# A transformer block with 32 routed experts on one core: gathers that wait for true block counts, zeroed result rows, earlier additions, fewer clears

## The reference

```python
x = x + cross_attention(layernorm(x), ctx, ctx)          # 16 heads of 16
xf = layernorm(x).reshape(4096, 256)
scores = sigmoid(xf @ gate_w.T)                          # 32 experts
# the best 4 of 8 groups by score + bias, then the best 6 experts within them
w = scores[chosen] / sum(scores[chosen]) * 2.5
routed = sum over the 6 chosen e of w[e] * (silu(xf @ gate_e.T) * (xf @ up_e.T)) @ down_e.T
x = x + routed + shared_ffn(xf)
```

## Time and profile before

| what | value |
|---|---|
| time, median of 3 runs | 761.74 us (759.81 to 762.38) |
| the profiled execution: its own time | 759.98 us |
| the profiled execution: span | 758.2 us |
| TensorE busy | 714.4 us (94%) |
| VectorE busy | 520.7 us (69%) |
| ScalarE busy | 394.2 us (52%) |
| GpSimd busy | 534.7 us (71%) |
| mean granted TensorE clock | 0.974 |

### The profile page before, as it was taken

One profiled execution on the slowest core, in us unless ns is written; L12 is line 12 of the kernel. 1 busy time (PEld: TensorE's weight loads), 2 busy tenths in 40 slices (PEclk: granted clock), 3 DMA queues, 4 the chain that ended last, 5 costly groups with the idle time before them and its releaser, 6 DMA issues.

```text
span 758.2 us, 18389 instructions
## 1 busy us (share of the span) xinstructions
PE 714.4 (94%) x5864; PEld 649.7 (86%) x5864; DVE 520.7 (69%) x1628; ACT 394.2 (52%) x836; POOL 534.7 (71%) x778
## 2 busy tenths in 40 slices
PE   6899999999999999998899999999999999999960
PEld 3789898888998888887589999999999999999950
DVE  4997777777777777776834327777776676676663
ACT  2455455455555555531046666666666666666630
POOL 0126778788888888878800027889888888888884
PEclk9999999999999999997999999999999999999995
DMA  9313443344342234334575557888888888888862
GB/s 277 109 57 113 127 139 109 122 140 136 137 141 80 82 112 139 135 126 144 171 228 197 168 178 243 261 269 263 272 269 274 274 269 264 262 276 269 282 202 81
DMA packets 97294, 140.13 MB, mean 185 GB/s; under 512 B 14943, under 2 KB 69731, under 8 KB 97200
## 3 DMA queue, kind: packets, MB, share of 16 engines
q1 hardware_dynamic: 77112, 87.50, 35.8%
q0 software_dynamic: 18432, 50.36, 21.5%
q10 hardware_dynamic: 1656, 1.10, 0.5%
HBM read 75.98 MB, written 62.94 MB: 183 GB/s over the span
## 4 chain that ended last, share of the span: by engine, by line
PE 75%; POOL 10%; DVE 6%; DMA 4%; issue 3%; DVEq 0%; POOLq 0%; ACT 0%; SPq 0%
PE sc_ps L989 19%; PE bank L1001 9%; PE bank L805 9%; PE sc_ps L865 7%; POOL work L550 6%; PE bank L793 5%; PE sc_ps L973 4%; PE bank L826 4%; PE bank L751 4%; DMA work<-yrows,dest 3%; PE sc_ps L771 3%; POOL work L503 3%; PE sc_ps L889 3%; PE sc_ps L767 2%; PE bank L835 2%
## 5 line engine op out<-in xcount | busy, mean ns | idle before, releaser
L513 POOL DMA_INDIRECT rows<-work,dest x192 | 188.3, 981 | 51.4 <-issue 26.9
L989 PE MATMUL sc_ps<-work 128*128 128x128 f32 x1792 | 218.6, 275 | 0.8 <-DVE work L1478 0.8
L550 POOL DMA_INDIRECT work<-yrows,dest x192 | 189.1, 985 | 34.9 <-POOL work L503 27.7
L989 PEld LDWEIGHTS sc_ps<-work 128*128 128x128 f32 x1792 | 209.1, 192 | 1.1 <-ACT work L655 1.0
L503 POOL MEMSET work<- 128x304 f32 (+1 forms) x350 | 133.1, 380 | 74.2 <-DMA yrows<-work 72.1
L1001 PE MATMUL bank<-wdn,work 128*128 x448 | 115.5, 380 | 0.6 <-DVE work L1433 0.6
L1459 DVE SCALAR_TENSOR_TENSOR work<-work 128x256 f32<-128x256 f32 x160 | 77.0, 482 | 47.1 <-DMA work<-yrows,dest 44.7
L1433 DVE TENSOR_TENSOR work<-work,sc_ps 128x256 f32<-128x256 f32 x112 | 46.9, 419 | 73.2 <-ACT work L660 73.1
L681 ACT ACTIVATE work<-bank 128x512 f32<-128x512 f32 x112 | 66.9, 597 | 54.3 <-PE bank L1001 54.3
L1001 PEld LDWEIGHTS bank<-wdn,work 128*128 128x128 f32 x448 | 76.6, 191 | 6.8 <-issue 1.0
L655 ACT ACTIVATE work<-sc_ps 128x512 f32<-128x512 f32 x112 | 66.3, 592 | 25.8 <-PE sc_ps L973 25.8
(11 more groups left out here) (168 smaller groups left out, 1051.7 us busy)
## 6 DMA issues: line engine op xcount, KB each, us to landing
work<-rows SPq DMA_DIRECT2D x224, 128.0 KB
yrows<-work SPq DMA_DIRECT2D x112, 256.0 KB
wgu<-in_egu SPq DMA_DIRECT2D x16, 512.0 KB, 4.2
store<-in_x SPq DMA_DIRECT2D x8, 512.0 KB, 11.1
wdn<-in_edn SPq DMA_DIRECT2D x8, 512.0 KB, 4.4
rows<-padrow SPq DMA_DIRECT2D x8, 512.0 KB, 3.3
out<-work SPq DMA_DIRECT2D x32, 128.0 KB
rows<-work,dest POOLq DMA_INDIRECT x192
```

The costliest lines, as they stand in the source:

```text
L513: pool.indirect_dma_start(rows[:, :], bass.IndirectOffsetOnAxis(ap=dest[:, t, k:k + 1], axis=0), rowb[:, m, :], None).then_inc(scat[m], 16)
L550: pool.indirect_dma_start(yg[:, g % RG, :], None, yrows[0:2 * n * P, :], bass.IndirectOffsetOnAxis(ap=dest[:, t, k:k + 1], axis=0)).then_i ...
L989: last = mm(ps8[2 + m % 2][:, (2 * w + g) * P:(2 * w + g + 1) * P], wst[w][m % 2][:, k * 2 * I + g * I:k * 2 * I + (g + 1) * I], xeT[:, m ...
```

## The change

There are five edits.

1. **True counts.** One more small matmul sums `begun` over the experts, and `count_stored` on VectorE turns it into `table` entries: for each tile and each of the 4 `y_st` semaphores the count that says that every block begun by the end of that tile is stored. GpSimd loads 16 of them (4 tiles) at a time (`load_known`), and waits on the four registers ahead of a tile's first gather. The waits by `stored_before` go; the row range that a gather may read is the same.
2. **Zeroed rows.** From tile 4 to tile 27 of the first part, SP stores 1 MB of zeros (8 blocks of 128 rows, `FILL`) into `yrows`, blocks 32 to 223. SP waits for these 24 stores ahead of the expert loop.
3. **Additions from pair 21** (ADD0), in place of 24.
4. **No clears** ahead of the gathers of tiles 16 to 31 (96 gathers; before, only the 6 of tile 31 had none).
5. `table`, `codes` and the PSUM bank hold a little more.

```diff
--- before.py
+++ after.py
@@ -30,13 +30,14 @@
 YP = 4
 PARTS = (0, 4, 16, NT)
 RG = 10
-ADD0 = 24
+ADD0 = 21
 OUT0 = ADD0 + 3
 NPR = NTB // 2
 UA, UB = 4, 8
 WORK = 13056
 TS = 8
 NPL = (NT - TS) // 2
+FILL0, FILL = 32, 8
 CLEARS = TOPK * NT - (NT - 4)
 NX = NT - TS
 
@@ -164,7 +165,7 @@
         padrow = sb("padrow", [P, D])
 
         pc = sb("pc", [P, 2, E * NT // P])
-        table = sb("table", [1, 4 * P], i32)
+        table = sb("table", [1, 4 * P + YP * NT], i32)
 
         att = []
 
@@ -248,7 +249,7 @@
         run, at = carve(work, at, [P, 2, 2 * NT])
         apart, at = carve(work, at, [P, NT])
         thr, at = carve(work, at, [P, NT])
-        codes, at = carve(work, at, [P, 2 * P])
+        codes, at = carve(work, at, [P, 2 * P + YP * NT])
         codes = codes[0:1, :].bitcast(i32)
         assert at <= 12 * 256 + 3 * NCH * P
 
@@ -271,6 +272,7 @@
         cum_ps = bank[3][0:E, 0:NT + 1]
         pos_ps = bank[3][0:E, 64:64 + NT]
         sch_ps = bank[3][0:1, P:P + NTB]
+        begun_ps = bank[3][0:1, P + NTB:P + NTB + NT]
         VB = (4, 6, 7, 4, 6)
         ps8 = [sc_ps[:, i, :] for i in range(4)] + [b[:, :] for b in bank]
         vchunk = [ps8[VB[c // 2]][:, (c % 2) * B * 3 * DH:(c % 2 + 1) * B * 3 * DH] for c in range(NCH)]
@@ -289,6 +291,7 @@
 
         scat = [sem(f"scat{i}") for i in range(4)]
         pads_st = sem("pads_st")
+        fill_st = sem("fill_st")
         ld_xe = [sem(f"ld_xe{i}") for i in range(RX)]
         y_st = [sem(f"y_st{i}") for i in range(YP)]
         ld_y = [sem(f"ld_y{i}") for i in range(RG)]
@@ -349,6 +352,12 @@
                 table[0:1, row * P + j:row * P + j + n], engines=(engine,), min_val=0, max_val=top,
                 skip_runtime_bounds_check_because="the table's entries are clipped to this range where it is made")
             return got
+
+        def load_known(t, n):
+            at = 4 * P + t * YP
+            _, got = nc.values_load_multi_w_load_instructions(
+                table[0:1, at:at + n * YP], engines=(mybir.EngineType.Pool,), min_val=16, max_val=16 * NPR // YP)
+            return [got[i * YP:(i + 1) * YP] for i in range(n)]
 
         def stored_before(t):
             return min(NPR, -(-(((t + 1) * P * TOPK + E * (P - 1)) // P) // 2))
@@ -400,9 +409,16 @@
                     sp.dma_start(ahead[0:P, e0:e0 + 4, :],
                                  padrow[:, :].unsqueeze(1).broadcast_to([P, 4, D])).then_inc(pads_st, 16)
 
+            def st_zeros(t, m, s):
+                b0 = FILL0 + FILL * (t - 4)
+                if FILL0 <= b0 < NTB:
+                    sp.dma_start(yrows[b0 * P:(b0 + FILL) * P, :].rearrange("(p j) d -> p j d", p=P),
+                                 padrow[:, :].unsqueeze(1).broadcast_to([P, FILL, D])).then_inc(fill_st, 16)
+
             def step(tile):
                 at_tile(tile, 0, ld_experts)
                 at_tile(tile, 0, st_pads)
+                at_tile(tile, 0, st_zeros)
             over_tiles(step)
 
             def ld_behind(i):
@@ -420,6 +436,7 @@
                 ld_behind(i)
             sp.wait_ge(S_["table"], 2)
             sp.wait_ge(pads_st, 16 * E // 4)
+            sp.wait_ge(fill_st, 16 * ((NTB - FILL0) // FILL))
             for one in scat:
                 sp.wait_ge(one, 16 * TOPK * NT // 4)
             sp.wait_ge(S_["gap"], CLEARS)
@@ -532,25 +549,26 @@
                 at_tile(tile, 0, late_inverse)
             over_tiles(step)
 
+            known = []
+
             def gather(t):
                 n = stored_before(t)
+                if t % 4 == 0:
+                    known.extend(load_known(t, 4))
                 need(pool, "dest2", t)
+                for one, stored_by in zip(y_st, known[t]):
+                    pool.wait_ge(one, stored_by)
                 for k in range(TOPK):
                     g = t * TOPK + k
-                    if g == 0:
-                        for i in range(n - YP, n):
-                            pool.wait_ge(y_st[i % YP], 16 * (i // YP + 1))
-                    elif k % 2 == 0 and n - 1 + k // 2 < NPR:
-                        i = n - 1 + k // 2
-                        pool.wait_ge(y_st[i % YP], 16 * (i // YP + 1))
                     if g >= RG:
                         need(pool, "part", g - RG)
-                    if t < NT - 1:
+                    if t < NT - 16:
                         gap(spare)
                     pool.indirect_dma_start(yg[:, g % RG, :], None, yrows[0:2 * n * P, :],
                                             bass.IndirectOffsetOnAxis(ap=dest[:, t, k:k + 1], axis=0)
                                             ).then_inc(ld_y[g % RG], 16)
             need(pool, "base", NPL - 1)
+            pool.wait_ge(S_["table"], 3)
             for t in range(NT):
                 gather(t)
 
@@ -944,6 +962,7 @@
 
             def number_blocks():
                 need(pe, "fresh", 0)
+                mm(begun_ps, const("ones")[0:E, 0:1], begun[0:E, 1:NT + 1], start=True, stop=True)
                 mm(pos_ps, const("tri")[0:E, 0:E], fresh[0:E, :], start=True, stop=False)
                 mm(pos_ps, const("ones")[0:E, 0:E], begun[0:E, 0:NT], start=False,
                    stop=True).then_inc(S_["pos_ps"], 1)
@@ -1380,6 +1399,15 @@
                 ts(table[:, 0:NTB], codes[:, 0:NTB], E - 1, None, ALU.bitwise_and).then_inc(S_["table"], 1)
                 ts(table[:, 2 * P:2 * P + NTB], codes[:, 0:NTB], 5, None, ALU.logical_shift_right).then_inc(S_["table"], 1)
 
+            def count_stored():
+                by_tile = codes[:, 2 * P:2 * P + YP * NT].rearrange("p (t r) -> p t r", r=YP)
+                for r in range(YP):
+                    ts(by_tile[:, :, r], begun_ps, float(2 * YP - 1), float(2 * YP - 1 - 2 * r), ALU.max,
+                       ALU.add).then_inc(S_["sch"], 1)
+                v.wait_ge(S_["sch"], 26 + YP)
+                ts(table[:, 4 * P:4 * P + YP * NT], codes[:, 2 * P:2 * P + YP * NT], 3, 4, ALU.logical_shift_right,
+                   ALU.logical_shift_left).then_inc(S_["table"], 1)
+
             def address_rows(i):
                 if i == 0:
                     v.wait_ge(S_["bc_ld"], 32)
@@ -1422,9 +1450,10 @@
             name_blocks()
             late_base(NPL - 4)
             read_table()
+            count_stored()
             for p in range(NPL - 3, NPL):
                 late_base(p)
-            v.wait_ge(S_["table"], 2)
+            v.wait_ge(S_["table"], 3)
             v.wait_ge(S_["ld_egu"], 16 * (E // 2))
 
             def hidden(i, m, q):
```

## The result

The changed kernel takes 752.32 us (median of 6 runs, 751.08 to 755.49), the kernel before 762.37 us (6 runs, 759.81 to 766.86): ratio 0.9875, 95% interval 0.9847 to 0.9903.

The account below looks back on a forecast made before the run. TensorE was taken to bound the loop, equal gather and addition paces the tail. -15.0 (tail) + 0.5 (loads) + 0.1 (extra matmul) = -14.4 us, so 747.3 us against the 761.74 median; range 744.5 to 752.5.

Parts of the forecast that it names:

- the term for the loads of counts: GpSimd ahead of every fourth tile: 1.5 us per load of 16 counts, between 0 and 2.6; 0.5 us entered as lost.
- What bounds the kernel: TensorE sets 3.089 us a pair; gathers every 1.553 us against 1.545 asked for leave 20 us of gathers and additions.
- VectorE's waits for gathers: Sign of being right: these waits are gone after tile 17, since gathers without clears run ahead of the additions.
- The first gather: Start of tile 0's gathers: near 441.7 us, with its lead over addition 0 staying 10.5 us.
- 4.0 spare and 2 borne: Gathers' lead at the start: 4.0 us beyond what is needed; TensorE bears additions about 2 us late.
- the first rival: GpSimd holds the first half through loads near 2.6 us or costly register waits: 750 to 756 us, chance 0.16.
- The waits on registers: GpSimd ahead of a tile's first gather: no cost for long-satisfied waits, 0.1 us each as the upper bound.
- No clears from tile 16: Later gathers take 1.25 us, 1.31 with a load's share; lateness is gone within a tile, then the ring rules.
- The tail: After the last pair: ten additions and weights end at 738.1, 5.15 us for the last store, end 743.2: -15.0 us.
- The zero stores: First part: 24 MB added, DMA share about 0.75, scatters with 8.4 us spare; 0 us entered.
- VectorE's gap: Before the expert loop: five short `count_stored` instructions fit where VectorE waits 1.06 us for TensorE; 0, or 0.5 if uncovered.
- its rival: Gathers collide with VectorE's copies, 4.5 us in place of 3.09 for two gathers: over 800 us, chance 0.01.

Follow-up runs that it names:

- constants: The changed kernel with GpSimd waiting for true counts written as constants, without the 8 loads of counts and their register instructions; right for these inputs alone: 744.29 us.
- loads ahead: The changed kernel with all its counts loaded once, ahead of tile 0, in GpSimd's idle time, one register a tile from tile 4 on: 744.09 us.
- the run with a late gather: The kernel with all counts loaded ahead of tile 0, plus one more gather behind the very last addition, whose rows nobody reads: 750.39 us, one run.

## Why the prediction was right in part, and where it was wrong

**The step that failed** is the term for the loads of counts: 1.5 us a load, at most 2.6, and from it 0.5 us lost by TensorE. The runs showed 3.4 to 4.2 us a load up to tile 12 and 9.1 us lost in the loop. That the time still lies within the range is luck. With 9.1 us lost the sum gives 755.9 us, outside the range; with the tail's measured 10.1 us in place of 12.0 as well, 754.0. The last 1.7 us are less than the 2.6 by which three runs of the kernel before differed, and no row shows their place.

**What bounds the kernel** held. TensorE sets the pace up to the last pair, GpSimd's and the additions' equal paces made the tail. With constants or loads ahead the loop runs at 3.089 us a pair and the tail is short. VectorE's waits for gathers were gone after tile 17, as forecast.

**The first gather** came 10.45 us ahead of its addition, as worked out (10.5), both later by the late start of the loop.

**The loads of counts.** The upper bound took a register instruction at SP's 37 ns; GpSimd's take 147 ns, with an assertion of 18 ns and the gaps 0.23 us a count. The idea that a gather covers part of a load holds in full for one load only, that of tile 20. By the prediction's own arithmetic, 3 x 4.2 + 96 x 0.008 = 13.4 us of lead against 4.0 spare and 2 borne gives 7.4 us lost; 9.1 was measured, and the arithmetic left out the load of tile 16, behind which the lead was 3.3 us. This was the first rival's mechanism (750 to 756 us, chance 0.16), with the share of the register instructions too small. Removing the loads gave the 8 us back; doubling them took 22 more. (The low end of the range, by its own words, is 744.8 and not 744.5; nothing hangs on it.)

**The waits on registers** cost nothing that can be seen: in the changed kernel, at tiles 9, 10, 13 and 14, where four such waits and no load stand ahead of the first gather, it comes 1.48 us behind the one before, the pace without waits. Constants gave 744.3 us, registers that are loaded ahead (44 waits in place of 128) 744.1.

**No clears from tile 16** held in its pace (gathers 1.25 us apart, 1.30 in the mean from tile 16 to 19), and in its use: the lead grew from 3.3 us at gather 96 to 14.2 at gather 162. Without it the change is slower than before (774.2 us), and with the loads ahead it is worth 6 us.

**The tail** was forecast at 12.0 us from the last `hidden` to the end and measured at 10.1. The additions were right but for a wait of 1.2 us for an output store, which I had not looked for. The 5.15 us that I put down to the last store was mis-sized: the span ends 2.2 us after the last addition, where the last gather is early enough. Before, the gather held the end: 758.2 - 749.74 = 8.46 us, as in the run with a late gather. The forecast thus missed 3 us of gain, of which the wait for the store took back one.

**The zero stores** were hidden, as entered: DMA share 0.73 in the stretch of the earlier trace rows, forecast at 0.75, and nothing waits.

```profile
150.00:200.00 50.00, 50.00 (x472) 44.86 (x470) 38.92 (x152) 26.59 (x62) 42.31 (x63) 1.00 0.73 240
```

`count_stored` fitted in VectorE's gap, less the last bit of it; the next addition of the shared part (line 1285) followed without idle time, and TensorE was not held:

```profile
377.56 0.49 DVE L1405 TENSOR_SCALAR work<-bank 1x32 int32<-1x32 f32 x4
378.08 0.42 DVE L1408 TENSOR_SCALAR table<-work 1x128 int32<-1x128 int32 x1
378.41 0.69 DVE L1285 TENSOR_TENSOR store<-sc_ps,wdn 128x512 f32<-128x512 f32 x1
```

**The late first pair** was not foreseen. TensorE's first gate-and-up group of 16 matmuls, before, and in the changed kernel with the transposes ahead of it:

```profile
386.44 2.14 PE L989 MATMUL sc_ps<-work 128*128 128x128 f32 x16 [0.75 <-DVE work L1478]
```

```profile
384.70 2.31 PE L992 MATMUL sc_ps<-cst,work 128*128 128x128 f32 x8 [2.87 <-DMA work<-rows]
...
387.78 3.75 PE L1008 MATMUL sc_ps<-work 128*128 128x128 f32 x16 [0.78 <-issue]
```

3.75 us in place of 2.14 for the same 16 matmuls. TensorE had stood idle for 2.9 us, waiting for the first blocks' rows, whose load waits for GpSimd's last scatter. Behind that idle time the granted clock (the third number from the end) fell to 0.50, the lower of its two levels, 1.2 GHz. The stretch of 388 to 390 us before, in the changed kernel, and in the kernel before without late clears:

```profile
388.00:390.00 2.00, 2.00 (x21) 2.00 (x20) 0.00 (x0) 1.97 (x4) 0.00 (x0) 1.00 0.88 267
```

```profile
388.00:390.00 2.00, 2.00 (x10) 2.00 (x11) 0.00 (x0) 1.92 (x3) 0.00 (x0) 0.50 1.04 342
```

```profile
388.00:390.00 2.00, 2.00 (x11) 2.00 (x11) 0.00 (x0) 0.23 (x1) 0.00 (x0) 0.50 0.84 252
```

With no zero stores the group is slow too:

```profile
387.37 3.36 PE L1005 MATMUL sc_ps<-work 128*128 128x128 f32 x16 [1.02 <-issue]
```

The kernel before without late clears, whose first part is unchanged, had pair 1 at 394.01 us, that with additions from 21 at 393.55. So the late start is no effect of the change: it comes with the lower clock in the old first part as well, and the one profile of before was an execution without it. What makes TensorE wait longer for the rows in some executions is not shown.

**The rule of the Trainium skill** (SBUF — State Buffer, section "SBUF: two separate sides") is that descriptors made by GpSimd wait while VectorE runs a two-port copy; it gives 3100 ns in place of 620 for one such DMA. In the changed kernel the longest of the 192 gathers took 1.23 us and the median 0.95, so no collision of the stated size shows here, and its rival fell. VectorE's copies beside them are short (0.49 us in the mean), and no run here has long ones beside gathers.

## What to carry to other kernels

A wait that gets a truer bound is worth little by itself where the waiting engine has no time to spare. Here fewer clears alone gave 6 us; true counts (loaded ahead) with the earlier start gave 12.6 us, and all three 19. The earlier start alone, without true counts, cost 72 us; by the program its wait closes a circle through the pipeline. When values are to be read into registers, count the register instructions at that engine's own price, and put them where the engine is idle. At the end of a program look at which engine's last work ends the span, also when the chain of waits names another.

## What was not expected of the hardware

- Register instructions on GpSimd's queue take 147 ns, on SP's 37 ns; reading 16 values into registers put 3.4 to 4.2 us between two gathers where clears stood between them, and nothing at tile 20, where the queue had read them six gathers early.
- An indirect gather keeps the program from ending for 8.4 to 8.7 us from its start, in eight profiles, though its data were added 2.8 us after its start.
- Additions that wait for gathers, 40 us in all and up to 2.4 us each, held TensorE for 5.3 us, where 34 us of such waits in the loop before, up to 2.0 us each, held it for 0.6. The totals are near each other, so they do not tell what TensorE loses; the reading is that it counts how far the additions fall behind.
